# Two requests for x in a two-layer graph kernel: lent slots swapped, one asked for earlier, one later

## What is computed

```python
h = einsum('bnf,fo->bno', x, W)                 # layer 0
e = h @ a1 + swapaxes(h @ a2, 1, 2)
e = where(e >= 0, e, 0.2 * e)
attention = softmax(adj * e, axis=1)
x = einsum('bij,bjo->bio', attention, h) + bias + x

support = einsum('bnd,df->bnf', x, W1) + b1     # layer 1
y = einsum('bnm,bmf->bnf', adj, support)
y = (y - mean(y, (0, 1))) * rsqrt(var(y, (0, 1)) + eps) * gamma + beta
return relu(y) + x
```

## Time and profile before

| | us |
|---|---|
| median of 3 runs | 900.86 |
| lowest and highest | 900.61, 905.04 |
| the profiled execution | 902.67 |
| its span, first to last instruction | 900.9 |
| PE busy | 858.1 |
| ACT busy | 809.5 |
| DVE busy | 777.9 |
| POOL busy | 200.5 |

### The profile page before, as it was taken

The page is one execution under the profiler, slowest core; times in us unless marked ns, Lnnn a source line. Parts: engine busy times, 40 slices in busy tenths (PEclk is TensorE's granted clock), DMA queues, the critical chain, the costliest instruction groups (busy, mean ns, idle before and its releaser), DMA issues.

```text
span 900.9 us, 9248 instructions
## 1 busy us (share of the span) xinstructions
PE 858.1 (95%) x3271; PEld 567.3 (63%) x3271; DVE 777.9 (86%) x846; ACT 809.5 (90%) x640; POOL 200.5 (22%) x168
## 2 busy tenths in 40 slices
PE   7999999999999999999999999999999999999960
PEld 5334666675666766676666766676666666666850
DVE  3664878989898989989898999989899898999966
ACT  5998789989998999999999899989999899998745
POOL 0102022203251133303331032501333033310000
PEclk9999999999999999999999999999999999999995
DMA  8998589888888789897998889897888978886988
GB/s 333 422 381 283 187 314 346 321 299 309 355 342 292 278 342 350 320 348 254 359 359 294 299 307 355 324 324 267 349 345 320 339 247 359 313 258 212 424 330 345
DMA packets 48525, 288.35 MB, mean 320 GB/s; under 512 B 5816, under 2 KB 6440, under 8 KB 15712
## 3 DMA queue, kind: packets, MB, share of 16 engines
q1 hardware_dynamic: 43584, 252.11, 72.9%
q0 software_dynamic: 4896, 35.65, 13.0%
HBM read 263.51 MB, written 24.23 MB: 319 GB/s over the span
## 4 chain that ended last, share of the span: by engine, by line
PE 79%; DMA 8%; ACT 6%; DVE 3%; issue 1%; SPq 1%; DVEq 0%; ACTq 0%
PE acc L576 31%; PE acc L545 9%; PE acc L549 9%; PE acc L543 9%; DMA adj_slot<-adjT 5%; PE acc L530 4%; PE acc L557 3%; ACT hi L706 3%; PE acc L504 3%; PE acc L590 2%; PE acc L592 2%; PE acc L595 2%; DMA adj_slot<-xT 2%; DVE scores L828 2%; PE acc L605 1%; PE acc L608 1%
## 5 line engine op out<-in xcount | busy, mean ns | idle before, releaser
L828 DVE CUSTOM_DVE_ANT_0 scores<-scores,adj_slot 128x2048 f32<-128x2048 f32 x128 | 296.7, 2318 | 59.2 <-DMA adj_slot<-adjT 30.5
L685 ACT ACTIVATE scores<-adj_slot,f_cols 128x2048 f32<-128x2048 f32 x128 | 255.4, 2002 | 17.4 <-PE acc L549 13.1
L864 DVE SCALAR_TENSOR_TENSOR exp_lo<-scores,rz,hi 128x2048 fp32r<-128x2048 f32 (+1 forms) x133 | 266.8, 2024 | 0.0
L692 ACT ACTIVATE scores<-scores,neg_mx 128x2048 f32<-128x2048 f32 x128 | 255.2, 1994 | 11.9 <-DVE neg_mx L831 11.9
L706 ACT ACTIVATE hi<-scores,rz 128x2048 fp32r<-128x2048 f32 (+1 forms) x133 | 227.9, 1733 | 20.3 <-DVE rz L840 20.2
L576 PE MATMUL acc<-adj_slot,region_even 128*128 128x512 f32 x400 | 178.9, 592 | 0.0
L576 PE MATMUL acc<-adj_slot,region_odd 128*128 128x512 f32 x296 | 132.6, 592 | 0.8 <-issue 0.8
L576 PEld LDWEIGHTS acc<-adj_slot,region_even 128*128 128x128 f32 x400 | 75.4, 189 | 77.5 <-issue 74.2
L549 PE MATMUL acc<-exp_lo,h_hi 128*128 128x512 f32 x448 | 120.4, 390 | 0.0
L545 PE MATMUL acc<-hi,h_hi 128*128 128x512 f32 x448 | 119.9, 389 | 0.0
L549 PEld LDWEIGHTS acc<-exp_lo,h_hi 128*128 128x128 f32 x448 | 83.5, 188 | 19.0 <-DVE exp_lo L864 1.9
(11 more groups left out here) (91 smaller groups left out, 800.7 us busy)
## 6 DMA issues: line engine op xcount, KB each, us to landing
adj_slot<-adjT SPq DMA_DIRECT2D x173, 1024.0 KB, 6.8
adj_lo<-adjT POOLq DMA_DIRECT2D x26, 1024.0 KB, 5.9
adj_slot<-xT SPq DMA_DIRECT2D x20, 1024.0 KB, 8.9
adj_slot<-biasT POOLq DMA_DIRECT2D x8, 1024.0 KB, 11.8
xp_dram<-adj_slot SPq DMA_DIRECT2D x32, 256.0 KB, 6.8
adj_slot<-xp_dram SPq DMA_DIRECT2D x8, 1024.0 KB, 12.2
adj_slot<-f_rows SPq DMA_DIRECT2D x7, 1024.0 KB, 7.3
adj_slot<-y_dram SPq DMA_DIRECT2D x7, 1024.0 KB, 12.3
```

Source lines behind the costliest of these rows:

```text
L685: act.activation(scores[t % ER][:, :], slots[f1_slot(bt.par)][:, :], ACT.Prelu, bias=f2_cols[:, bt.n, t:t + 1], alpha=ALPHA).then_inc(edge ...
L692: act.activation(scores[e][:, :], scores[e][:, :], ACT.Exp, bias=neg_mx[:, e:e + 1], accum_out=zsum[:, e:e + 1]).then_inc(exp_done, 1)
L828: dve.tensor_tensor_reduce(scores[e][:, :], scores[e][:, :], slots[s][:, :], 1.0, NEG_BIG, ALU.mult, ALU.max, mx[:, e:e + 1]).then_inc(max ...
L864: dve.scalar_tensor_tensor(exp_lo[e][:, part_cols(t, i)], scores[e][:, part_cols(t, i)], rz[:, e:e + 1], hi[m][:, part_cols(t, i)].bitcast ...
```

## The change

The roles of tiles 10 and 11 are traded: T_RES is 10 and T_X is 11, and RELOAD keeps the places 5 and 6 for tiles 10 and 11. Through k = T_RES + 1 the residual x is asked for at k = 11 (was 12), ahead of adj tile 14; through k = T_X + 2 x for h is asked for at k = 13 (was 12), behind adj tile 15. In batch 0 the residual is asked for between the stores of f_rows and the wait for them.

```diff
-    T_F, T_HI, T_X, T_RES = 8, 9, 10, 11
+    T_F, T_HI, T_RES, T_X = 8, 9, 10, 11
...
-    RELOAD = {T_F: 3, T_HI: 4, T_X: 5, T_RES: 6}
+    RELOAD = {T_F: 3, T_HI: 4, T_RES: 5, T_X: 6}
...
                     sp.wait_ge(row_out, 1)
                     for c in range(NC):
                         sp.dma_start(f_rows[:, cols(c)], f_sb[QF * c:QF * c + NF, :]).then_inc(f_stored, 16)
+                    load_residual(bt)
                     sp.wait_ge(f_stored, 16 * NC)
                     sp.dma_start(f2_grid, f_rows[B - 1:NF].rearrange("b (t p) -> (b t) p", p=P)).then_inc(f2_loaded, 16)
                     sp.wait_ge(h_mm, NC)
                     load_adj(nx, 0)
                     load_adj(nx, 1)
                     load_f1(nx)
-                    load_residual(bt)
```

## The result

| | before | after |
|---|---|---|
| median, us (22 runs each) | 902.30 | 899.36 |
| lowest, highest | 899.02, 906.72 | 896.70, 903.61 |
| ratio, 95% interval | | 0.9969 (0.9956 to 0.9981) |
| profiled execution | 902.67 | 900.12 |
| its span | 900.9 | 898.3 |

The change gains 2.9 us of the 14.2 forecast, and 899.4 is above the range's head of 895. The gain of batch 0 is there. That of the batch ends, 9.9 us in the sum, is not.

The account below looks back on a forecast made before the run. PE bounds the kernel, held up by the bias in batch 0 and adj tile 15 at the ends of batches 1 to 6. 900.86 less 14.2 (4.3 in batch 0, 9.9 at batch ends) gives 886.6 us, range 884 to 895.

Parts of the forecast that it names:

- Reading what bounds the kernel: PE has 79% of the chain; it idles 2.67 us in batch 0 and 9.94 us at ends of batches 1 to 6.
- (a): Lent slots: tiles 10 and 11 trade roles, their slots having been read long before; cost nothing.
- (b): Batch 0, x asked for ahead of the wait for the rows: 2.6 us of idle plus 1.7 of clock, 4.3 us gained.
- the clock: Batch 0, L557 after PE's idle: without the idle it takes 3.73 instead of 5.47 us, 1.74 us gained.
- (c): Batches 1 to 7, x for the sum asked for one tile earlier, ahead of adj 14, bias 6.4 us earlier: no cost.
- (d): Batches 1 to 6, x for h after adj 15: adj 15 lands in 5.2 to 6.4 us, 9.9 us gained.
- C: Rival: the bias holds adj 14, batch ends keep their excess, only batch 0 gains; 896.4 us, 10%, half counted as no change.
- F: Rival: requests move but no wait does, because the waits named have other causes; 900.9 us, 2%.
- theory 1: From the experiments: DMA engines serve SP's and POOL's requests roughly in arrival order; the adding bias costs two plain loads' work.

Follow-up runs that it names:

- e3: Kernel before with one edit: x for h asked for at k = 13, behind adj 15, instead of k = 12; 895.11 us, ratio 0.9902.
- e6: Changed kernel, but from batch 1 on POOL asks for the bias only when adj 15 has landed; 890.97 us, ratio 0.9847.
- e2: Changed kernel with batch 0's request for x for the sum put back where it was; 903.34 us, ratio 0.9997.
- e5: Kernel before with x for the sum of batch 0 ahead of the wait for the rows and x for h at k = 13; 891.96 us, ratio 0.9866.
- e7: Changed kernel with x for h one place later, at k = 14, behind the next batch's first tile; 899.33 us, ratio 0.9957.
- e1: Kernel before with only batch 0's edit, x for the sum asked for ahead of the wait for the rows; 899.88 against 903.99 us, ratio 0.9961.

## Why the prediction was wrong, step by step

**Reading what bounds the kernel: right.** The excess of 9.94 us and its cause, adj 15, are confirmed: e3 and e6 bring DVE's wait at tile 15 and PE's excess to nothing together, and e6 gains 1.5%.

**(a), slots: right** as far as the traces can tell; no new wait stands at tiles 10 or 11.

**(b), batch 0: right in mechanism, a little too large.** Edited kernels take 32.7 to 33.4 us for the part in the table (six traces, mean 33.0), unedited ones 34.7 to 38.1 (four, mean 36.6): 3.6 us in place of 4.3. The term that was mis-sized is the clock. In the four unedited ones L557 took 5.47 and 5.20 us (before), 5.47 (e2, idle 1.91 us ahead of it) and 3.84 (e3, idle 1.83 us). The granted clock from 92 to 94 is 0.57, 0.50, 0.71 and 1.00 in this order. So the clock is lost in some executions and not in all, and 1.7 us is a price that is not always paid: the mean of the four is 1.2 us over the 3.84 of the edited ones. The bias lands in 8.24 us where 8.26 was taken, and at 82.08 less the 2.64 us of the later start it is asked for at 79.4, as forecast.

**(c), x for the sum one tile earlier: the step that failed.** The prediction took from rows 8 that a bias can take at most 3.6 us from a neighbour, the difference of two landings, and that "the bias starts 1 to 2 us behind adj 14: at no cost". Its cost to the neighbour is its DMA work, 5.4 to 5.6 us. And the neighbour is adj 15, not adj 14: adj 14 landed in 5.1 us, the bias ran behind it and held the next request. The difference of landings understates the work, since a landing of an adj tile in 4.7 us holds about 2 us (4.7 less the 2.7 below) that are no transfer. The profile of before had it; part 3 of its page:

```profile
q1 hardware_dynamic: 43584, 252.11, 72.9%
q0 software_dynamic: 4896, 35.65, 13.0%
```

252.11 MB are 240 loads of 1 MB, and 0.729 x 900.9 / 240 is 2.7 us each; POOL's 0.130 x 900.9 = 117.1 less 26 such loads leaves 46 us for eight biases, 5.7 each. With that, and the prediction's 2.5 us for a load, the sum would have read: work ahead of adj 15 before, adj 14 and two x, 3 x 2.5 = 7.5 us; after, adj 14 and the bias, 2.5 + 5.6 = 8.1. No gain.

**(d), x for h later: right alone, wrong in this change.** "It lands 5.2 to 6.4 us after its request": 4.7 in e3 and 4.8 with the bias held back (e6), 7.8 as the change stands. The allowance of 1.2 us for the rest of the bias was the failure of (c) over again.

**Before, most of the bias had been behind adj 15.** The prediction read the lateness of adj 15 as queue plus bias beside it. The stretches of before, 430 GB/s at 172 to 174 and

```profile
178.00:180.00 2.00, 2.00 (x10) 1.66 (x9) 1.68 (x1) 2.00 (x2) 0.54 (x1) 1.00 1.00 291
180.00:182.00 2.00, 2.00 (x10) 1.68 (x9) 0.31 (x1) 2.00 (x2) 0.00 (x0) 1.00 0.98 193
182.00:184.00 2.00, 2.00 (x6) 0.95 (x6) 1.99 (x2) 0.69 (x2) 0.00 (x0) 1.00 1.02 242
```

show its slow traffic only from 179 or so on, though POOL asked at 175.48. Until then SP's queue has the engines; from 174 to 179 it moved

```profile
q1 hardware_dynamic: 279, 2.02, 101.5%
```

and POOL's queue nothing. From 179 to 182 POOL's queue moved 0.35 MB, and from 181 to 183, with SP's loads done, 0.39 MB. So at the landing of adj 15, 7.5 us after 174.06, at most a third of the bias had run. What made adj 15 late before was mostly the 3 MB of SP's own loads ahead of it; the change took two of them away and put the bias in their place.

**The rivals.** C came nearest in size at the batch ends (no gain there, 10%), but had the bias hold adj 14; it held adj 15, one request further. By the time alone F's 900.9 is nearest to 899.4, but F has no wait move, and that of batch 0 did. The rule of the Trainium skill behind it ("DMA: Bandwidth & Descriptors", section "Queues, rings and completion order"), turns between the queues by packets, was given as what speaks against the change. The runs agree with its outcome in that SP's order does not protect a tile from POOL's queue, but for adj 15 and not for adj 14. The end of batch 1 looks like order of arrival: adj 14, asked for 1.3 us ahead of the bias, was not late, and adj 15, asked for 5 us behind, got nothing while the bias ran and landed 3.0 us later than in e6. In e3 the two queues do take turns. There the bias was asked for 1 us behind x for h, and from 178 to 184 they moved

```profile
q0 software_dynamic: 103, 0.84, 68.2%
q1 hardware_dynamic: 104, 0.72, 30.4%
```

one packet of the profile against one. What decides between the two pictures stays open, so theory 1 holds for the stretch that matters here and is not shown as a general rule. The prediction put 89% on a gain that can be told from no change; had the two x loads and the bias been weighed as work, no gain at the batch ends would have had the largest share.

## What to carry to other kernels

Weigh a transfer that others queue behind by the DMA work it costs, the queue's share of the engines times the span over its number of transfers, and not by its landing time; here an adding transfer cost twice a copy. Before moving a request earlier, list all that it releases: here x pulled the bias along, and the bias came to stand ahead of the one tile that is waited for. Two moves that are each good by their own row may cancel, so they are to be summed in one list of what is ahead of the critical request.

## What had not been expected of the hardware

The adding transfer of 1 MB onto SBUF costs 5.4 to 5.6 us of the 16 DMA engines, about 2.7 more than a copy, and the rate falls to 197 to 238 GB/s at a full share while it runs, against 397 and 426 beside it. While it runs (172 to 175 in after), a plain load of another queue got nothing at all.

The start of the program varies by 2 to 3 us from one execution to the next: the last L489 group starts between 59.05 and 59.56 in five traces and between 61.19 and 62.27 in seven. PE's timeline, first before, then after:

```profile
15.94 4.33 PE L504 MATMUL acc<-w_sb,adj_slot 128*128 128x128 f32 x24
21.26 3.67 PE L530 MATMUL acc<-scores,hi_x 128*128 128x512 f32 x8 [0.99 <-issue]
```

```profile
16.89 2.92 PE L504 MATMUL acc<-w_sb,adj_slot 128*128 128x128 f32 x24
22.21 5.37 PE L530 MATMUL acc<-scores,hi_x 128*128 128x512 f32 x8 [2.40 <-issue]
```

In the one L504 is slow and the L530 behind it fast, in the other the reverse, after a longer idle. The granted clock falls at different places: to 0.50 from 18 to 20 us before, to 0.62 and 0.52 from 22 to 26 after. A slow L504 is made up for by a shorter idle behind it (0.99 against 2.40 us), a slow L530 is not.

The later start is not spread evenly: six of seven traces with the traded slots have it, and one of five without. So a cost of the traded slots at the start is a rival that the traces don't rule out. The medians speak against it: with the same edit of batch 0 and hardly any excess, the traded e6 is not slower than the untraded e5 (0.9847 and 0.9866), nor e7 slower than e1 (0.9957 and 0.9961) at like excess. Both kinds occur with and without the traded slots (e5 and e7 against e1 and after), so it is taken as a property of the execution; the runs don't prove it.
